# Attention scores of one key tile: queries meet keys and their rests in one 256-column product

## What is computed

```python
x = x + 0.5 * ffn(layernorm(x))
x = x + attn(layernorm(x))           # x: 2 x 512 x 512
x = x + 0.5 * ffn(layernorm(x))

# attn: 32 query heads, 8 key/value heads, head size 128, so G = 4 query heads to one key head
q, k = rmsnorm(q, q_norm_w), rmsnorm(k, k_norm_w)
scores = einsum('bkgqd,bksd->bkgqs', q, k) / sqrt(128)
bias = where(rel > 0, -1e30, slopes * rel)   # rel = key position - query position
out = einsum('bkgqs,bksd->bkgqd', softmax(scores + bias), v)
```

## Time and profile before

| | us |
|---|---|
| median of 3 runs | 1240.72 |
| lowest and highest | 1239.37, 1241.39 |
| the profiled execution | 1239.88 |
| its span, first to last instruction | 1238.6 |

### The profile page before, as it was taken

The page is one execution under the profiler, slowest core; times in us unless marked ns, Lnnn a source line. Parts: engine busy times, 40 slices in busy tenths (PEclk is TensorE's granted clock), DMA queues, the critical chain, the costliest instruction groups (busy, mean ns, idle before and its releaser), DMA issues.

```text
span 1238.6 us, 18593 instructions
## 1 busy us (share of the span) xinstructions
PE 1217.7 (98%) x6418; PEld 1067.7 (86%) x6418; DVE 827.4 (67%) x2002; ACT 757.3 (61%) x1760; POOL 649.4 (52%) x526
## 2 busy tenths in 40 slices
PE   6999999999999999999999999999999999999999
PEld 5788888899998999999999999999999778888887
DVE  7966665776666677567667667677677768655555
ACT  4454442357677777777767767767767774544442
POOL 4686561744675625725724724824824343765550
PEclk9999999999999999999999999999999999999999
DMA  6142232212213122122122122122122010221101
GB/s 232 40 156 106 105 104 102 93 44 86 70 51 103 43 77 102 41 80 95 43 85 94 43 86 94 44 86 87 51 86 77 26 51 19 63 74 52 52 17 68
DMA packets 33452, 93.77 MB, mean 76 GB/s; under 512 B 4112, under 2 KB 4784, under 8 KB 31312
## 3 DMA queue, kind: packets, MB, share of 16 engines
q1 hardware_dynamic: 33120, 92.29, 21.6%
q10 hardware_dynamic: 240, 0.30, 0.1%
HBM read 62.69 MB, written 29.88 MB: 75 GB/s over the span
## 4 chain that ended last, share of the span: by engine, by line
PE 90%; DVE 5%; ACT 2%; POOL 1%; issue 1%; DMA 1%; SPq 0%; DVEq 0%; ACTq 0%; POOLq 0%
PE bank L345 21%; PE bank L347 21%; PE bank L346 20%; PE bank L590 5%; PE bank L424 4%; PE bank L430 4%; PE bank L425 4%; PE bank L604 3%; PE bank L609 3%; PE bank L605 3%; PE bank L569 2%; DVE stats L1081 1%; PE bank L572 1%; PE bank L373 1%; DVE probT_l L1357 0%
## 5 line engine op out<-in xcount | busy, mean ns | idle before, releaser
L961 ACT ACTIVATE prob<-prob,neg_top 128x128 f32<-128x128 f32 (+3 forms) x256 | 141.1, 553 | 78.6 <-DVE neg_top L1346 78.0
L1603 POOL TENSOR_TENSOR rows<-rows,row_root_y 128x640 f32<-128x640 f32 x64 | 80.7, 1261 | 205.0 <-DVE row_root_y L1077 205.0
L1597 POOL TENSOR_TENSOR square<-rows 128x640 f32<-128x640 f32 x64 | 79.4, 1256 | 161.0 <-DVE rows L1382 125.1
L970 ACT ACTIVATE prob<-prob,inverse 128x128 f32<-128x128 f32 (+3 forms) x256 | 123.0, 553 | 5.5 <-DVE inverse L1351 5.5
L1472 POOL TENSOR_TENSOR w_l_late<-raw_late,w_h_late 128x512 fp32r<-128x512 f32 (+1 forms) x59 | 90.4, 1549 | 68.2 <-ACT w_h_late L718 68.2
L1357 DVE TENSOR_TENSOR probT_l<-bank,probT_h 128x512 fp32r<-128x512 f32 x160 | 101.4, 683 | 22.2 <-ACT probT_h L976 22.1
L976 ACT CAST probT_h<-bank 128x512 fp32r<-128x512 f32 x160 | 84.5, 595 | 43.0 <-PE bank L590 43.0
L1346 DVE CUSTOM_DVE_ANT_0 prob<-bank,bias 128x128 f32<-128x128 f32 (+3 forms) x256 | 109.7, 484 | 0.0
L345 PE MATMUL bank<-o_h,oT_h 128*128 128x512 f32 x256 | 105.6, 413 | 4.0 <-DVE oT_l L1363 4.0
L1142 DVE SCALAR_TENSOR_TENSOR x_rows<-bank,x_rows 128x512 f32<-128x512 f32 x112 | 75.7, 687 | 45.8 <-PE bank L430 45.8
L347 PE MATMUL bank<-o_h,oT_l 128*128 128x512 f32 x256 | 101.4, 396 | 0.0
(11 more groups left out here) (213 smaller groups left out, 3751.6 us busy)
## 6 DMA issues: line engine op xcount, KB each, us to landing
x_ring<-x_between SPq DMA_DIRECT2D x64, 256.0 KB, 2.6
x_between<-x_ring SPq DMA_DIRECT2D x56, 256.0 KB, 2.0
raw_late<-w_qkv SPq DMA_DIRECT2D x8, 1536.0 KB, 6.5
raw_early<-ffn_w SPq DMA_DIRECT2D x21, 512.0 KB, 4.1
scaled<-raw_early SPq DMA_DIRECT2D x21, 512.0 KB, 2.7
raw_late<-scaled SPq DMA_DIRECT2D x21, 512.0 KB, 3.8
raw_late<-w_o SPq DMA_DIRECT2D x8, 1024.0 KB, 5.1
x_between<-x_rows SPq DMA_DIRECT2D x8, 256.0 KB, 2.0
```

The lines of the kernel that those rows point to most:

```text
L961: last = act.activation(p, p, ACT.Exp, bias=neg_top[:, h:h + 1], scale=-1.0, accum_out=total[:, h:h + 1])
L970: act.activation(p, p, ACT.Copy, scale=inverse[:, h:h + 1]).then_inc(prob_done, 1)
```

## The change

kT_h and kT_l become the two halves of one tensor kT, so that one access covers the 128 rounded keys and their 128 rests. For units with one tile of keys a head's scores are two matmuls: qT_h with 256 columns (keys and rests), whose result is 256 wide, then qT_l with the 128 rounded keys, added to the left half. Two heads share a bank (4 x 128 columns), so a unit takes two banks. VectorE first adds the bias to the right halves (the rests' part), in one `tensor_tensor` of 128 x 256 for each bank, into prob; then, after waiting for its own writes, does the four reductions as before, with prob in the place of the bias. A bank is released after its second head, and the exponentials of both heads wait for that. Units with more keys stay as they are.

```diff
-        kT_h, kT_l = sb("kT_h", [S], F32R), sb("kT_l", [S], F32R)
+        kT = sb("kT", [2, S], F32R)
+        kT_h, kT_l = kT[:, 0, :], kT[:, 1, :]
...
+                if keys == P:
+                    for h in range(0, G, 2):
+                        r, bank = result("scores", n, h)
+                        for head in (h, h + 1):
+                            cols = (head - h) * 2 * P
+                            pe.matmul(bank[:, cols:cols + 2 * P], qT_h[:, head, :], kT[:, :, 0:P], start=True, stop=False,
+                                      skip_group_check=True)
+                            last = pe.matmul(bank[:, cols:cols + P], qT_l[:, head, :], kT_h[:, 0:P], start=False, stop=True,
+                                             skip_group_check=True)
+                        last.then_inc(full[r.bank], 1)
+                    return
...
             def exponentials(n, heads):
-                    r = results["scores", n, h]
+                    r = results["scores", n, h - h % 2 if keys == P else h]
...
             def scores(n):
+                if keys == P:
+                    two = [results["scores", n, h] for h in range(0, G, 2)]
+                    for h, r in zip(range(0, G, 2), two):
+                        dve.wait_ge(full[r.bank], r.nth)
+                        rests = banks[r.bank][:, :].rearrange("p (h m c) -> p h m c", h=2, m=2)[:, :, 1, :]
+                        own_step(dve.tensor_tensor(prob[:, h:h + 2, 0:P], rests, bias[:, h:h + 2, S - P:S], ALU.add))
+                    for h in range(G):
+                        r = two[h // 2]
+                        if h == 0:
+                            own_wait()
+                        last = dve.tensor_tensor_reduce(prob[:, h, 0:P], banks[r.bank][:, h % 2 * 2 * P:h % 2 * 2 * P + P],
+                                                        prob[:, h, 0:P], -(2.0 ** -g), -MASKED, ALU.add, ALU.min, neg_top[:, h:h + 1])
+                        if h % 2:
+                            last.then_inc(evac[r.bank], 1)
+                    return
```

## The result

The changed kernel takes 1242.78 us in the median of ten executions (1242.44 to 1245.2), the one before 1239.57 (1238.9 to 1241.39). The ratio is 1.0028 with a 95% interval of 1.002 to 1.0036: slower by about 0.3%. The medians are 3.2 us apart where +3.7 was forecast. The forecast of the time itself, 1244.4, is 1.6 us above the measured one; 1.15 of this is its base, a median of three executions (1240.72) that came to 1239.57 with ten. The profiled execution took 1242.86 us with a span of 1241.2.

What follows compares the result with a forecast made beforehand. PE was taken to bound the kernel (90% of the chain), with VectorE's path through oT_h becoming the bound in usual slots. Terms 3.4 - 0.84 + 0.64 + 0 + 0.50 = +3.7 us on 1240.72 gave 1244.4 us, range 1240.0 to 1248.0.

Steps and rivals of the forecast that it cites:

- eleven usual slots: Attention units 16, 20, ... 56 (t = 0, one tile of keys): each +0.31 us, together +3.4 us.
- units 4 and 8: Longer attention slots with 3.4 us of slack at kT_l: PE is the bound, 2 x -0.42 = -0.84 us.
- units 0 and 1: Start of attention: unit 0 gets the full 1.00 us delay, unit 1's 0.36 wait for probT_h goes, +0.64 us.
- unit 12: Attention slot where VectorE's slow row_root_y swallows a start 0.45 later: 0, up to +0.45 us if not.
- unit 60: Attention slot where PE waits 0.85 us for oT_l itself; ScalarE's slack about 0.50: +0.50 us.
- The chain: Usual slot: VectorE's later scores delay exponentials, then oT_h, VectorE's block to kT_l and PE's next scores, +0.31 us.
- first exponential: ScalarE in a usual slot: starts 3.3 us behind the slot's start instead of 2.31.
- 0.7 us lost by steps at the head of the next slot: PE at the head of t = 1 slots: waits 0.73 us for VectorE's qT_l or kT_l.
- the block behind oT_h: VectorE's work from oT_l to kT_l without idle time, 5.7 us, hung on ScalarE's oT_h.
- D: Delay of a slot's first exponential from VectorE's additions and the pair's common bank release: 1.00 us, bounds 0.72 to 1.26.
- The slack arithmetic: In general a t = 0 slot changes by D - 0.69 us, but never below -0.42.
- the 0.36 of idle time: Unit 1: PE's wait for probT_h, expected to go, leaving 1.00 - 0.36 = +0.64 us.

Runs made afterwards that it cites:

- e1: Changed kernel without its two VectorE additions, the reductions taking the bias as before: 1232.54 us, ratio 0.9949 to the kernel before.
- e2: Changed kernel with PE back at three 128-column score matmuls a head, VectorE's part kept: 1243.61 us, ratio 1.0033 to the kernel before.
- e4: Changed kernel with two sums of squares moved ahead of the reciprocal in usual t = 0 slots: 1236.2 us, ratio 0.9968 to the kernel before.
- e5: Changed kernel in which each pair's reductions wait for their own addition alone: 1241.02 us, ratio 1.0012.
- e8: Changed kernel with VectorE going pair by pair (addition, wait, two reductions): 1239.32 us, ratio 1.0001.
- e3: Kernel before, with two sums of squares moved ahead of the reciprocal in usual t = 0 slots: 1239.66 us, ratio 1.0001.
- e7: Changed kernel with a third 128 x 256 addition, into a tile nothing reads: 1247.22 us, ratio 1.0061.
- e9: Changed kernel with pair-by-pair order, even heads released by their own reduction, and sums of squares moved early: 1235.11 us, ratio 0.9963 to the kernel before.
- e6: Changed kernel in which an even head's exponential is released by its own reduction through a separate semaphore: 1239.46 us, ratio 1.0001.

## Why the prediction was right, step by step

| step | forecast | measured in the two profiles |
|---|---|---|
| eleven usual slots | 11 x +0.31 = +3.4 | 11.02 to 11.31 (0.27 to 0.29 more each), +3.1 |
| units 4 and 8 | -0.84 | 12.09 to 11.67 each, -0.84 |
| units 0 and 1 | +0.64 | 17.83 to 18.03, +0.20 |
| unit 12 | 0 | 11.69 to 11.72 |
| unit 60 | +0.50 | 8.95 to 9.49, +0.55 |
| units 61 and 62 | 0 | 19.67 to 18.40, -1.27 |
| unit 30 | 0 | 11.25 to 11.46, +0.21 |

The chain was right as named: PE's scores 0.95 us (0.93 forecast), first exponential at 3.31 (3.3), no idle time ahead of oT_h, 0.7 us lost by steps at the head of the next slot, slots of 11.3. e1 and e2 separate its halves, e4 shows that the block behind oT_h carries it, and e5 to e8 that D is its measure with slope 1. The slack arithmetic came out 0.03 to 0.04 high in four of the five cases in which VectorE's path sets the slot, 0.02 in the other; in the changed kernel most of it is the cast oT_h, which takes 0.57 us where 0.59 was carried over from before. The rows that the forecast had a number or a zero for, the last two left out, add up to +3.0 against +3.7.

**Mis-sized: units 0 and 1.** The full 1.0 us arrived in unit 0 (6.54 to 7.56), but unit 1 gave back 0.82, not 0.36. The prediction took the 0.36 of idle time in the earlier trace rows for the wait. By steps the kernel before lost more there. PE, kernel before:

```profile
276.08 0.28 PE L347 MATMUL bank<-kT_h,qT_l 128*128 128x256 f32 x1
...
277.03 0.40 PE L605 MATMUL bank<-probT_h,v_l 128*128 128x512 f32 x1
277.36 0.50 PE L609 MATMUL bank<-probT_l,v_h 128*128 128x512 f32 x1
277.69 0.34 PE L345 MATMUL bank<-w_h_late,xnT_hi 128*128 128x384 f32 x1
```

The same stretch after the change:

```profile
277.86 0.28 PE L349 MATMUL bank<-kT,qT_l 128*128 128x256 f32 x1
277.98 0.40 PE L619 MATMUL bank<-probT_h,v_h 128*128 128x512 f32 x1
278.21 0.39 PE L620 MATMUL bank<-probT_h,v_l 128*128 128x512 f32 x1
278.44 0.39 PE L624 MATMUL bank<-probT_l,v_h 128*128 128x512 f32 x1
278.67 0.34 PE L347 MATMUL bank<-w_h_late,xnT_hi 128*128 128x384 f32 x1
```

From the last score matmul to the first of the projection it was 1.61 us (276.08 to 277.69) and is 0.81 (277.86 to 278.67): 0.80 was lost, of which the bracket showed 0.36. The rest is the modelled length of the matmul before, and steps of 0.31 to 0.33 in place of 0.23 behind it.

**Not foreseen.** The profile of before had lost 1.3 us in units 61 and 62 to PE's clock (last section), and that of after hadn't. Ahead of the attention, the first unit's scores began at 268.16 and 268.92: PE waited 0.8 us longer for the first normalised rows (the second wait in the list above; 2.9 us before), where no line was changed and where the eleven profiles range from 267.12 to 268.92. The account of the profiled executions, 2.98 us apart, is then: 0.76 ahead of the attention, 1.91 in it, next to nothing behind it, and the last 0.3 outside the span. So what the forecast had no term for came to about zero by luck: -1.27 of the clock against 0.76, 0.22 of unit 30 and 0.3. Without the clock's fall the attention alone would be 3.2 us longer, which is also the difference of the medians; that both agree so well is partly luck too, as the ten executions of the changed kernel lie up to 2.8 us apart, and those of the kernel before in one set 5.3 (1237.77 to 1243.04).

Unit 30, t = 2 and untouched, is 0.2 us longer in all profiles but those of before, e1, e3 and e7. VectorE of the changed kernel there:

```profile
631.48 0.56 DVE L1412 TENSOR_TENSOR rows<-bank,rows 128x384 f32<-128x384 f32 x1 [0.26 <-issue]
...
632.61 0.28 DVE L1353 TENSOR_TENSOR kT<-bank,kT 128x128 fp32r<-128x128 f32 x1
```

Ahead of add_products VectorE stands idle for 0.26 us with nothing that the profile shows to wait for ("issue"). In the four profiles without the longer slot this idle time isn't there. kT_l lands at 632.89, and PE's next scores start 0.10 behind it, at 632.99, as at the head of the t = 1 slots. Why VectorE pauses stays open.

## What to carry over

Work taken from the bounding engine is worth only what the path that meets it next leaves of it. Here that path, VectorE's scores, the exponentials and the block behind oT_h, had 0.69 us of slack a slot (0.50 at oT_h, 0.19 at kT_l). With D = 0.22 on it all of the 0.42 saved came through (e1); the change put D = 1.00 on it, ahead of that very meeting point. So look first for the other path's slack, then for what can leave the block behind the meeting point (two sums of squares, 1.5 us, moved into idle time, turned the loss into a gain). And size a wait on a pipelined engine by the step between starts, not by the idle time in brackets, which understated it by 0.24 to 0.44 us here.

## What the runs showed of the hardware

**The price of a short matmul isn't its own.** Forecast were steps of 0.12 for 256 columns and 0.11 for 128. The sum of a pair is right, 0.23, but the parts are 0.17 (458.64 to 458.81 in the changed kernel) from the wide one to the short one and 0.06 (458.58 to 458.64) from the short one to the next. So the next matmul can start 0.06 us behind one of 128 columns, where twelve of them in a row took 0.11 each. What sets these steps, loading of weights or another thing, wasn't tested.

**PE's clock can fall in one execution and not in the next, with the same idle time ahead.** The kernel before, in stretches (us, busy us and instructions of each engine, granted clock, DMA):

```profile
984.00:987.00 3.00, 1.45 (x10) 1.03 (x8) 3.00 (x12) 1.91 (x7) 3.00 (x3) 1.00 0.34 87
987.00:989.00 2.00, 1.57 (x6) 1.24 (x7) 1.52 (x11) 1.75 (x7) 0.36 (x1) 0.84 0.00 0
989.00:991.00 2.00, 2.00 (x6) 1.59 (x5) 1.80 (x9) 2.00 (x6) 0.58 (x1) 0.50 0.00 0
```

And the changed kernel, 4 us later in its span:

```profile
988.00:991.00 3.00, 1.39 (x10) 0.97 (x8) 3.00 (x12) 1.97 (x7) 3.00 (x3) 1.00 0.33 93
991.00:993.00 2.00, 1.62 (x7) 1.36 (x8) 1.52 (x11) 1.75 (x7) 0.22 (x1) 1.00 0.00 0
993.00:995.00 2.00, 2.00 (x15) 1.71 (x13) 1.79 (x9) 2.00 (x6) 0.63 (x1) 1.00 0.00 0
```

In both PE idles for 2.0 us ahead of project_out in unit 61 (first row the kernel before, second the changed one):

```profile
987.43 0.50 PE L345 MATMUL bank<-o_h,oT_h 128*128 128x512 f32 x1 [1.98 <-DVE oT_l L1363]
...
991.38 0.50 PE L347 MATMUL bank<-o_h,oT_h 128*128 128x512 f32 x1 [1.99 <-DVE oT_l L1393]
```

In the first its granted clock then stands at 0.50, the lower of its two levels (1.2 of 2.4 GHz), matmuls of 512 columns step by 0.43 instead of 0.23 us, and the slot takes 10.13 us instead of 8.74. Of the eleven profiles six show the fall in this slot (before, e3, e4, e7, e8, e9) and five don't (after, e1, e2, e5, e6). It is worth 1.3 us after what the next slot gives back, almost half of what this study set out to measure. The executions on record show about the same size: of the 54 of the kernel before that ran beside the experiments, the 30 with a mean granted clock of 1.000 have a median of 1239.04, the 24 below it one of 1240.20. The ten of the changed kernel split into four and six, with 1242.56 and 1243.71, so the change costs about 3.5 us at either clock. Such falls are one reason to compare slots rather than spans. What decides whether the clock falls wasn't tested.
